# Expert weights split in five pieces a block over 13 blocks instead of eight pieces a block over 8

## The chip, the cores and the metric

One NeuronCore of a Trainium2 chip runs the kernel. The metric is the device time of one execution in microseconds (us), as the median over several executions. A profile is one further execution with the hardware profiler on.

## What is computed

An input x of 16 batches, 256 time steps and 256 features passes four residual layers, x = x + layer(x):

- L0, a tanh recurrence over the time steps: h = tanh(h Wh + x Wx + b)
- L1, an LSTM over the time steps, with four gates of 256
- L2, a mixture of experts: a shared two-matrix feed-forward (256 to 1024 to 256, gelu between) for all, and for each batch the two best of E = 4 experts of the same shape, weighted and masked by segment of time
- L3, an adapter whose low-rank factors w = gelu(c W1 + bias1) W2 + bias2 are generated for each batch from a condition (the "generator"; W2 is 256 by 8192), and that then transforms x

Every fp32 matrix is split into a high and a low fp16 part, and each product is three fp16 products (high by high, low by high, high by low).

## The kernel before

The engines have separate programs, unrolled, which synchronise by semaphores. The sequence of 256 time steps is cut in NB = 16 blocks of U = 16 windows. Window u of block `it` holds one LSTM step, the L0 step of the next block, the input products of later gates (`fig_x`, `o_x`), and a share of the shared feed-forward of block it-1 by the list `FILL`: `shared_hidden` ("h") of tiles 0 to 7 in windows 1, 1, 3, 5, 7, 9, 11, 13, `shared_down` ("d") in the even windows from 2 on. From window to window the LSTM is a loop through three engines: TensorE (PE) makes the gates (L1268, L1274), ScalarE (ACT) takes tanh (L530, L534), VectorE (DVE) updates the cell (L837, L838, L840), ACT takes tanh of the cell (L541), DVE makes the new state (L842), and PE waits for it.

Weights are prepared in the spare time of these windows. SyncE (SP) loads a 1 MB fp32 matrix into a staging buffer. For each piece of 256 columns ACT writes the high part (`weight_hi`, L490) and DVE the low part (`weight_lo`, L722, which then raises the semaphore `v_wlo`). `stage[0]` takes, one after another, the LSTM's first matrix, the shared `sw1` and the eight expert matrices E0 to E7 (`ew1` and `ew2` of four experts, eight pieces each, 64 in all). So expert matrix j can be loaded only when the last piece of matrix j-1 is split. `stage[1]` takes `sw2` and then the eight parts of W2, part j for block j+1: PE multiplies it in windows 12 and 13 (`low_rank`, L1314), DVE adds the bias in window 14 (`add_bias`, which raises `v_low`).

In blocks 1 to 8 one expert matrix a block is split, in windows 2, 4, 5, 6, 7, 9, 11 and 12. ACT waits for the matrix before the first piece of each. All programs are in order: what stands behind a waiting instruction on an engine waits too. In a window ACT has, in order, gate tanh, L0 tanh, cell tanh, refills of gate banks by the bias (`seeds`, in windows 3, 7, 11, 15), gelu (`shared_gelu`, odd windows), a rounding of x (windows 4, 6), and then the piece.

SP's program after the shared matrices is: E0, four bias loads and W2 part 0; then for j = 1 to 7 a wait for the end of W2 part j-1 (`pe_w2`, `v_low`: window 14 of block j), four bias loads (L337), W2 part j (L340), and right behind it E j (L326), whose pieces are by then free. Then, after all splits (`ALL_SPLIT`), the adapter's base matrices and 96 small stores of the generated factors to a scratch in HBM. PE waits for all pieces of the shared matrices (`SHARED_SPLIT`) between block 0 and block 1.

After the 16 blocks come the last shared tiles, the routed experts (which need all expert pieces), and the adapter.

Of the kernel before, what the change touches and what calls it, by code (L numbers as in the profile page):

```python
# [28 lines left out]
C = D // P  # L29
U = 16  # L30
NB = T // U
G = 8
H = 4
E = 4
SHARED = E
F = 1024
M = F // P
# [20 lines left out]
def build_program(nc, a, out, scratch):  # L58
    ctx = ExitStack()
    with ctx:  # L60
# [173 lines left out]
            return stage[0][:, at], S_W1, part_(HI), part_(LO)  # L234


        EXPERT_WINDOWS = (2, 4, 5, 6, 7, 9, 11, 12)

        def x_tiles(half, i):

# [42 lines left out]
        @block.sync  # L283
        def _(sp):
            with nc.allow_non_contiguous_dma(reason="small tables, once"):
                sp.dma_start(cond[:, :], a["cond_1024"]).then_inc(s["ld_cond"], 16)
                wide = lambda w: w.rearrange("(c p) n -> p c n", p=P)

                def load_x(half, quarter):

                    some = slice(4 * quarter, 4 * quarter + 4)
                    sp.dma_start(xin[:, half, some, :], a["x"][some, half * P:(half + 1) * P, :].rearrange("b t d -> t b d")
                                 ).then_inc(s[f"ld_x{half * 4 + quarter}"], 16)

                for quarter in range(4):
                    load_x(0, quarter)
                for w, name in enumerate(("L0_cond_Wx", "L0_cond_Wh")):
                    sp.dma_start(rnn_raw[:, w], wide(a[name])).then_inc(s["ld_rnn"], 16)
                sp.wait_ge(s["g_const"], 3)
                for row in (0, 32):  # L300
                    sp.dma_start(bias_rows[row:row + 1, 0:4 * D],
                                 a["L1_cond_b"].rearrange("(a n) -> a n", a=1)).then_inc(s["ld_bias"], 16)
                    sp.dma_start(bias_rows[row:row + 1, 4 * D:5 * D],
                                 a["L0_cond_b"].rearrange("(a n) -> a n", a=1)).then_inc(s["ld_bias"], 16)
                for w, name in enumerate(("L1_cond_Wx", "L1_cond_Wh")):
                    sp.dma_start(stage[w][:, :].rearrange("p (c n) -> p c n", c=C), wide(a[name])
                                 ).then_inc(s[f"ld_stage{w}"], 16)
                for quarter in range(4):
                    load_x(1, quarter)
                for i, tile in enumerate(FIG_TILES + O_TILES):  # L310
                    sp.dma_start(gate_bias[:, i:i + 1], a["L1_cond_b"][tile * P:(tile + 1) * P].rearrange("(p o) -> p o", o=1)
                                 ).then_inc(s["ld_gate_bias"], 16)
                small_tables(sp)
                sp.wait_ge(s["v_wlo"], N_RNN + N_LSTM // 2)
                sp.dma_start(stage[0][:, :].rearrange("p (c n) -> p c n", c=C), wide(a["L2_cond_sw1"])
                             ).then_inc(s["ld_stage0"], 16)
                sp.wait_ge(s["v_wlo"], LSTM_SPLIT)
                sp.dma_start(stage[1][:, :].rearrange("p (m n) -> p m n", m=M), wide(a["L2_cond_sw2"])
                             ).then_inc(s["ld_stage1"], 16)

                for j in range(2 * E):
                    def load_expert():

                        sp.wait_ge(s["v_wlo"], SHARED_SPLIT + j * N_MATRIX if j else LSTM_SPLIT + N_MATRIX)
                        src = a[("L2_cond_ew1", "L2_cond_ew2")[j % 2]][j // 2]
                        sp.dma_start(stage[0][:, :].rearrange("p (c n) -> p c n", c=(C, M)[j % 2]), wide(src)  # L326
                                     ).then_inc(s["ld_stage0"], 16)

                    if j == 0:
                        load_expert()  # L330
                        sp.wait_ge(s["v_wlo"], SHARED_SPLIT)
                    else:
                        sp.wait_ge(s["pe_w2"], j)
                        sp.wait_ge(s["v_low"], j)
                    for t in range(4):
                        at = j * 1024 + t * LOW_N
                        sp.dma_start(low_bias[32 * t:32 * t + 32, :],  # L337
                                     a["L3_cond_bias2"][at:at + LOW_N].partition_broadcast(2 * B)
                                     ).then_inc(s["ld_bias2"], 16)
                    sp.dma_start(w2_in, wide(a["L3_cond_W2"])[:, :, j * 1024:(j + 1) * 1024]  # L340
                                 ).then_inc(s["ld_stage1"], 16)
                    if j > 0:
                        load_expert()
                sp.wait_ge(s["v_wlo"], ALL_SPLIT)
                for dst, name in ((down, "L3_cond_base_down"), (up, "L3_cond_base_up")):
                    sp.dma_start(dst, wide(a[name])).then_inc(s["ld_updown"], 16)

                sp.wait_ge(s["a_low"], Q * C)
                sp.wait_ge(s["v_lowlo"], Q * C)
                for g in range(Q * C):  # L350
                    for place, h in enumerate((HI, LO, HI) if g // C in LEFT else (HI, HI, LO)):
                        for t in range(4):
                            at = g % C * P + t * LOW_D
                            dst = scratch[place, :, g // C, at:at + LOW_D].rearrange("(b r) d -> b r d", r=R)
                            sp.dma_start(dst, rows[32 * t:32 * t + B, h, g]).then_inc(s["st_scratch"], 16)
                sp.wait_ge(s["st_scratch"], N_SCRATCH)

            def load_low(b, r):
                sp.dma_start(low[r], scratch[:, bass.ds(b * R, R), :, :].rearrange("h r q d -> h r (q d)")
                             ).then_inc(s[f"ld_low{r}"], 16)  # L360

            def store_out(b, slot):
                sp.wait_ge(s["a_out"], b * 2 + 2)
                sp.dma_start(out[bass.ds(b, 1), :, :].rearrange("o (k p) d -> p (o k) d", p=P),
                             y4[:, slot]).then_inc(s[f"st_out{slot}"], 16)

            def step(b, r, prev, this, next1, next2):
                if not isinstance(b, int) or b + 4 < B:
                    sp.wait_ge(s["pe_e1"], b + 1)
                    load_low(b + 4, r)  # L370
                if prev:
                    store_out(b - 1, (r + 1) % 2)

            for b in range(4):
                load_low(b, b)
            adapter_steps(sp, step)
            for slot in range(2):
                sp.wait_ge(s[f"st_out{slot}"], 16 * (B // 2))
# [98 lines left out]
        def _(act):  # L477
# [9 lines left out]
            def weight_hi(piece):  # L487

                view, scale, hi, _lo = piece
                nc.scalar.activation(hi, view, ACT.Copy, scale=scale).then_inc(s["a_whi"], 1)  # L490
# [101 lines left out]
            def block_steps(it, first, last, matrix=False):  # L592
                for u in range(U):
# [16 lines left out]
                        weight_hi(shared_piece(i))  # L610
                    if matrix and u == HI_WINDOW:
                        low_hi(it - 1)
                    if matrix and u in EXPERT_WINDOWS:
                        i = EXPERT_WINDOWS.index(u)
                        if i == 0:
                            act.wait_ge(s["ld_stage0"], it * 16 + 32)
                        weight_hi(expert_piece(it - 1, i))

            def low_hi(g):

# [77 lines left out]
        def _(dve):  # L698
# [247 lines left out]
            def block_steps(it, first, last, xr, matrix=False):  # L946
                for u in range(U):
# [13 lines left out]
                        add_bias(it - 1)  # L961
                    if matrix and u == LO_WINDOW:
                        low_lo(it - 1)
                    if matrix and u in EXPERT_WINDOWS:
                        i = EXPERT_WINDOWS.index(u)
                        weight_lo((it - 1) * N_MATRIX + (SHARED_SPLIT + i), expert_piece(it - 1, i))
                    if xr and u in X_LO:
                        x_lo(it + 2, X_LO.index(u))
                    if last and u == U - 4:
# [196 lines left out]
        def _(pe):  # L1166
# [126 lines left out]
            def shared_hidden(blk, m):  # L1293
                tile = blk * M + (M + m)
                def free():
                    if m == 0:
                        pe.wait_ge(s["v_x2p"], blk * 2 + (4 if blk == NB - 1 else 2))
                    pe.wait_ge(s["a_g"], tile - 1)
                hidden(tile, lambda h, c: SW1[:, h, c, m * P:(m + 1) * P],
                       lambda h, c: XHL[:, h, c, :, bass.ds(blk * U, U)], HB[m % 2], free)  # L1300

            def shared_down(blk, m):
                if m == 0:
                    pe.wait_ge(s["v_y"], blk + 1)
                down_(blk * M + (M + m), m, lambda h, c: SW2[:, h, m, c * P:(c + 1) * P],
                      m == 0, m == M - 1, YB)

# [129 lines left out]
                    rnn_x(it + 2)  # L1437

            block_steps(0, True, False, True)
            pe.wait_ge(s["v_wlo"], SHARED_SPLIT)  # L1440
            for it in range(1, 2 * E + 1):
                block_steps(it, False, False, True, matrix=True)
            for it in range(2 * E + 1, NB - 2):
# [161 lines left out]
```

## Time and profile before

| what | value |
|---|---|
| median of 3 runs | 1182.06 us (1181.74 to 1182.39) |
| profiled execution, its own time | 1186.63 us |
| profiled execution, span from first to last instruction | 1184.8 us |
| PE busy | 1136.6 us, 96% |
| DVE busy | 766.9 us, 65% |
| ACT busy | 608.0 us, 51% |
| mean granted TensorE clock | 0.960 |
| expert loads: 8 of 1024 KB, median time from issue to landing | 8.6 us |
| W2 loads: 8 of 1024 KB, the same | 5.4 us |

The 1.8 us between span and time of the profiled execution lie outside its instructions. Its time is 4.6 us over the median of the runs.

### The profile page before, as it was taken

How to read it: one execution, taken by the hardware profiler on the slowest of the kernel's cores; microseconds unless marked ns; L12 is line 12 of the kernel's file. 1: busy time of each engine (PE TensorE's matmuls, PEld its weight loads, DVE VectorE, ACT ScalarE, POOL GpSimd, SP SyncE). 2: the span in 40 equal slices, each digit the busy share in tenths (PEclk: the TensorE clock that was granted, in tenths of full speed). 3: DMA queues.
4: the chain of work that ended last, by engine and by line, in shares of the span. 5: the costliest groups of instructions: out<-in, count | busy, mean ns of one | idle time of the engine just before them, and what ended most of it. 6: DMA issues, size and time to landing. Idle time of an engine off the chain costs nothing. (4 is left out here: it accounts for less than half of the span.)

```text
span 1184.8 us, 58156 instructions
## 1 busy us (share of the span) xinstructions
PE 1136.6 (96%) x23706; PEld 1014.0 (86%) x23706; DVE 766.9 (65%) x2954; ACT 608.0 (51%) x2147; POOL 364.4 (31%) x1372
## 2 busy tenths in 40 slices
PE   5899999999999999999999999899999999999898
PEld 4788888888889888999999998678888888888687
DVE  6566666666666666565565657687666666666697
ACT  4456566566566565555565554533333333333476
POOL 3654344344434344444444440063000000000121
PEclk7759999989989999999999999899999999999899
DMA  8211202202102011110000000000000000000022
GB/s 243 74 44 39 79 4 80 79 4 79 53 31 79 29 54 26 14 15 12 5 4 4 5 4 4 3 1 2 2 2 2 2 1 2 2 2 2 5 75 86
DMA packets 44432, 37.14 MB, mean 31 GB/s; under 512 B 24280, under 2 KB 39946, under 8 KB 44172
## 3 DMA queue, kind: packets, MB, share of 16 engines
q1 hardware_dynamic: 43564, 33.12, 9.2%
q8 instruction: 194, 3.18, 1.1%
q14 instruction: 66, 0.54, 0.2%
q10 hardware_dynamic: 608, 0.30, 0.1%
HBM read 28.42 MB, written 4.98 MB: 28 GB/s over the span
## 5 line engine op out<-in xcount | busy, mean ns | idle before, releaser
L1268 PEld LDWEIGHTS bank<-LH,seq 128*128 128x128 f16 x8192 | 248.8, 96 | 54.0 <-DVE LH L842 46.5
L1268 PE MATMUL bank<-LH,seq 128*128 128x16 f16 x8192 | 283.1, 170 | 12.3 <-DVE LH L842 10.3
L568 ACT ACTIVATE gel<-bank,seq 128x256 f32<-128x256 f32 x256 | 121.5, 475 | 215.0 <-PE bank L1173 211.3
L1171 PE MATMUL bank<-XHL,WE 128*128 128x256 f16 x768 | 210.6, 274 | 5.7 <-issue 2.9
L1171 PE MATMUL bank<-GH,WE 128*128 128x256 f16 x768 | 210.6, 274 | 2.2 <-DVE GH L815 1.8
L1172 PE MATMUL bank<-XHL,WE 128*128 128x256 f16 x768 | 210.7, 274 | 0.0
L1173 PE MATMUL bank<-XHL,WE 128*128 128x256 f16 x768 | 210.7, 274 | 0.0
L1172 PE MATMUL bank<-GH,WE 128*128 128x256 f16 x768 | 210.7, 274 | 0.0
L1173 PE MATMUL bank<-GH,WE 128*128 128x256 f16 x768 | 210.6, 274 | 0.0
L1274 PE MATMUL bank<-LH,seq 128*128 128x16 f16 x4096 | 177.2, 169 | 2.3 <-issue 2.3
L399 POOL TENSOR_TENSOR RH<-rf,RH 128x32 f16<-128x32 f32 x256 | 64.6, 252 | 355.9 <-ACT RH L525 355.9
L530 ACT ACTIVATE tfig<-bank 128x96 f32<-128x96 f32 x256 | 65.8, 257 | 210.4 <-PE bank L1274 208.2
L822 DVE CAST GH<-gel 128x256 f16<-128x256 f32 x256 | 78.3, 306 | 103.7 <-ACT gel L568 102.9
L1274 PEld LDWEIGHTS bank<-LH,seq 128*128 128x128 f16 x4096 | 139.5, 96 | 1.6 <-issue 1.6
L1172 PE MATMUL bank<-seq 128*128 128x64 f16 (+2 forms) x960 | 138.6, 207 | 1.4 <-issue 1.4
L1173 PE MATMUL bank<-seq 128*128 128x64 f16 (+2 forms) x960 | 139.7, 207 | 0.0
L1171 PE MATMUL bank<-seq 128*128 128x64 f16 (+2 forms) x960 | 137.1, 206 | 0.0
L469 POOL TENSOR_TENSOR seq<-X,seq 128x512 f16<-128x512 f32 x16 | 19.3, 1205 | 342.2 <-ACT seq L643 342.2
L837 DVE SCALAR_TENSOR_TENSOR fc<-tfig,c 128x32 f32<-128x32 f32 x256 | 48.9, 191 | 114.8 <-ACT tfig L530 109.5
L824 DVE TENSOR_TENSOR GH<-gel,GH 128x256 f16<-128x256 f32 x256 | 113.0, 441 | 8.7
L842 DVE SCALAR_TENSOR_TENSOR LH<-to,tc 128x32 f16<-128x32 f32 x256 | 51.7, 202 | 78.3 <-ACT tc L541 78.3
L1173 PEld LDWEIGHTS bank<-seq 128*128 128x128 f16 x960 | 91.4, 100 | 2.8 <-issue 1.5
(193 smaller groups left out, 2539.6 us busy)
## 6 DMA issues: line engine op xcount, KB each, us to landing
stage<-in_L_cond_ew SPq DMA_DIRECT2D x8, 1024.0 KB, 8.6
stage<-in_L_cond_W SPq DMA_DIRECT2D x8, 1024.0 KB, 5.4
XHL<-in_x SPq DMA_DIRECT2D x8, 512.0 KB, 9.0
out<-WE SPq DMA_DIRECT2D x16, 256.0 KB, 2.1
stage<-in_L_cond_sw SPq DMA_DIRECT2D x2, 1024.0 KB, 5.5
scratch<-rows SPq DMA_DIRECT2D x96, 8.0 KB, 2.3
stage<-in_L_cond_Wx SPq DMA_DIRECT2D x1, 1024.0 KB, 9.1
stage<-in_L_cond_Wh SPq DMA_DIRECT2D x1, 1024.0 KB, 11.3
```

Of the source, the lines that this page charges most:

```text
L399: nc.gpsimd.tensor_tensor(RH[:, slot, LO], rf[:, slot], RH[:, slot, HI], ALU.subtract).then_inc(s["p_rlo"], 1)
L530: nc.scalar.activation(tfig[:], FIG[u // H % 2][:, 0:6 * H * B].rearrange("p (m t b) -> p m t b", m=6, t=H)[:, :, u % H, :], ACT.Tanh, sca ...
L568: nc.scalar.activation(gel[:, m % 2, :], banks[m % len(banks)][:, 0:256], ACT.Gelu_apprx_tanh, scale=scale, bias=bias).then_inc(s["a_g"], 1)
L822: V.tensor_copy(GH[:, m % 4, HI], gel[:, m % 2]).then_inc(s["v_gh"], 1)
L824: V.tensor_tensor(GH[:, m % 4, LO], gel[:, m % 2], GH[:, m % 4, HI], ALU.subtract).then_inc(s["v_gl"], 1)
L837: V.scalar_tensor_tensor(fc[:], tf, 1.0, c2[:], ALU.add, ALU.mult)
L842: V.scalar_tensor_tensor(hh, to[:], 1.0, tc[:], ALU.add, ALU.mult).then_inc(s["v_hh"], 1)
L1171: MM(out_, w(HI), x(HI), start=start, stop=False, skip_group_check=True)
L1172: MM(out_, w(LO), x(HI), start=False, stop=False, skip_group_check=True)
L1173: return MM(out_, w(HI), x(LO), start=False, stop=stop, skip_group_check=True)
L1268: MM(z, LW[:, h, 1, c, tile * P:(tile + 1) * P], LH[:, old, HI, c], start=False, stop=False, skip_group_check=True)
L1274: last = MM(z, LW[:, HI, 1, c, tile * P:(tile + 1) * P], LH[:, old, LO, c], start=False, stop=(c == C - 1), skip_group_check=True)
```

## The change

`EXPERT_WINDOWS` becomes (2, 4, 7, 9, 11): the pieces of windows 5, 6 and 12 are gone, and the 64 pieces are numbered through. Piece i is split in block i // 5 + 1, window `EXPERT_WINDOWS[i % 5]`, so blocks 1 to 12 have five pieces each and block 13 has four. A matrix ends in the middle of a block. ACT waits for a new one before each piece i with i % 8 == 0.

SP's order is built by a loop over blocks: expert matrix j stands ahead of the W2 part of the block in which its first piece can be split. The order is E0, W0, W1, E1, W2, W3, E2, W4, E3, W5, W6, E4, W7, E5, E6, E7 (Wj: part j of W2 with its bias loads). The waits of each load are unchanged: E j for the last piece of E j-1, W j for the use of W j-1.

PE's wait for both shared matrices between blocks 0 and 1 is taken out. `shared_hidden` of block 0 waits for the first (`LSTM_SPLIT + N_MATRIX`), `shared_down` of block 0 for the second.

```diff
-        EXPERT_WINDOWS = (2, 4, 5, 6, 7, 9, 11, 12)
+        EXPERT_WINDOWS = (2, 4, 7, 9, 11)
+        PIECES = 2 * E * N_MATRIX
...
-                for j in range(2 * E):
-                    def load_expert():
+                def load_expert(j):
...
-                    if j == 0:
-                        load_expert()
                         sp.wait_ge(s["v_wlo"], SHARED_SPLIT)
...
-                    if j > 0:
-                        load_expert()
+                loaded = 0
+                for it in range(NB - 1):
+                    while loaded < 2 * E and (loaded * N_MATRIX - 1) // len(EXPERT_WINDOWS) + 1 <= it:
+                        load_expert(loaded)
+                        loaded += 1
+                    if it < 2 * E:
+                        load_low_matrix(it)
...
-                    if matrix and u in EXPERT_WINDOWS:
-                        i = EXPERT_WINDOWS.index(u)
-                        if i == 0:
-                            act.wait_ge(s["ld_stage0"], it * 16 + 32)
-                        weight_hi(expert_piece(it - 1, i))
+                    if it > 0 and u in EXPERT_WINDOWS:
+                        i = (it - 1) * len(EXPERT_WINDOWS) + EXPERT_WINDOWS.index(u)
+                        if i < PIECES:
+                            if i % N_MATRIX == 0:
+                                act.wait_ge(s["ld_stage0"], i // N_MATRIX * 16 + 48)
+                            weight_hi(expert_piece(i // N_MATRIX, i % N_MATRIX))
...
+                            weight_lo(SHARED_SPLIT + i, expert_piece(i // N_MATRIX, i % N_MATRIX))
...
+                    if blk == 0 and m == 0:
+                        pe.wait_ge(s["v_wlo"], LSTM_SPLIT + N_MATRIX)
...
+                    if blk == 0:
+                        pe.wait_ge(s["v_wlo"], SHARED_SPLIT)
...
             block_steps(0, True, False, True)
-            pe.wait_ge(s["v_wlo"], SHARED_SPLIT)
```

## Rows read from the trace of the kernel before

**Rows 1.** Windows by block 2, 7, 8, 10: length, busy, clock, DMA share, GB/s.

```profile
core 0: us, PE busy (x) PEld busy (x) DVE busy (x) ACT busy (x) POOL busy (x), PEclk, DMA share, GB/s
136.30:183.60 47.30, 45.18 (x1262) 40.58 (x1259) 29.82 (x138) 27.67 (x114) 19.26 (x80) 0.96 0.16 51
...
370.10:414.70 44.60, 44.16 (x1262) 39.76 (x1259) 29.83 (x137) 27.66 (x114) 19.01 (x80) 1.00 0.15 54
414.70:461.90 47.20, 44.30 (x1261) 39.81 (x1258) 29.82 (x137) 27.64 (x114) 18.99 (x80) 1.00 0.14 46
...
504.70:547.40 42.70, 42.53 (x1244) 39.60 (x1241) 25.49 (x127) 24.56 (x104) 18.95 (x80) 1.00 0.12 18
```

**Rows 2.** Timeline of SP: start, duration, load.

```profile
85.36 1.72 SPq L337 DMA_DIRECT2D low_bias<-in_L_cond_bias  x4
...
131.23 1.71 SPq L337 DMA_DIRECT2D low_bias<-in_L_cond_bias  x4
132.98 0.43 SPq L340 DMA_DIRECT2D stage<-in_L_cond_W  x1
133.46 0.47 SPq L326 DMA_DIRECT2D stage<-in_L_cond_ew  x1
178.48 1.80 SPq L337 DMA_DIRECT2D low_bias<-in_L_cond_bias  x4
...
223.96 2.84 SPq L337 DMA_DIRECT2D low_bias<-in_L_cond_bias  x4
...
271.91 3.08 SPq L337 DMA_DIRECT2D low_bias<-in_L_cond_bias  x4
...
317.33 2.03 SPq L337 DMA_DIRECT2D low_bias<-in_L_cond_bias  x4
...
365.07 1.72 SPq L337 DMA_DIRECT2D low_bias<-in_L_cond_bias  x4
...
409.65 1.73 SPq L337 DMA_DIRECT2D low_bias<-in_L_cond_bias  x4
```

**Rows 3.** Waits of PE from 93 to 460 us: total, times, longest.

```profile
PE bank L1171 <- issue: 2.5, 1, 2.5
...
PE bank L1248 <- issue: 1.7, 1, 1.7
```

**Rows 4.** DMA queues from 131 to 138.4 us, then from 138.4 to 140.5 us.

```profile
DMA packets 739, 1.46 MB, mean 198 GB/s; under 512 B 80, under 2 KB 483, under 8 KB 739
...
q1 hardware_dynamic: 739, 1.46, 69.7%
...
q8 instruction: 1, 0.02, 2.8%
```

**Rows 5.** Waits of PE's weight loads for the LSTM state, from 93 to 460 us.

```profile
PEld bank L1268 <- DVE LH L842: 22.3, 73, 0.7
```

**Rows 6.** Timeline of PE at the first LSTM step of block 1.

```profile
90.26 0.82 PE L1268 MATMUL bank<-LH,seq 128*128 128x16 f16 x24
```

**Rows 7.** Timeline of DVE, starts of windows 5 and 11, block 7 and block 10.

```profile
383.24 0.19 DVE L837 SCALAR_TENSOR_TENSOR fc<-tfig,c 128x32 f32<-128x32 f32 x1 [0.42 <-ACT tfig L530]
...
399.06 0.19 DVE L837 SCALAR_TENSOR_TENSOR fc<-tfig,c 128x32 f32<-128x32 f32 x1 [0.34 <-ACT tfig L530]
...
517.77 0.19 DVE L837 SCALAR_TENSOR_TENSOR fc<-tfig,c 128x32 f32<-128x32 f32 x1 [0.96 <-ACT tfig L530]
...
532.97 0.19 DVE L837 SCALAR_TENSOR_TENSOR fc<-tfig,c 128x32 f32<-128x32 f32 x1 [0.44 <-ACT tfig L530]
```

**Rows 8.** Issues of the expert loads from 66 to 70 us: E0 alone.

```profile
DMA to landing us min/median/max: 5.6/5.6/5.6
```

**Rows 9.** Timelines of DVE and ACT, block 2: end of window 7, window 9.

```profile
159.97 0.42 DVE L722 SCALAR_TENSOR_TENSOR WE<-stage,WE 128x256 f16<-128x256 f32 x1
...
164.64 0.41 ACT L490 ACTIVATE WE<-stage 128x256 f16<-128x256 f32 x1
164.95 0.25 ACT L530 ACTIVATE tfig<-bank 128x96 f32<-128x96 f32 x1
```

**Rows 10.** The same in block 7: end of window 2, window 4.

```profile
377.40 0.44 DVE L722 SCALAR_TENSOR_TENSOR WE<-stage,WE 128x256 f16<-128x256 f32 x1
...
381.96 0.40 ACT L490 ACTIVATE WE<-stage 128x256 f16<-128x256 f32 x1
382.96 0.25 ACT L530 ACTIVATE tfig<-bank 128x96 f32<-128x96 f32 x1 [0.59 <-PE bank L1274]
```

More of the change, by code:

```diff
@@ L319, in _, with load_low_matrix @@
                              ).then_inc(s["ld_stage1"], 16)
-                for j in range(2 * E):
-                    def load_expert():
[L324 to L327, printed above, removed]
+                def load_expert(j):
+                    sp.wait_ge(s["v_wlo"], SHARED_SPLIT + j * N_MATRIX if j else LSTM_SPLIT + N_MATRIX)
+                    src = a[("L2_cond_ew1", "L2_cond_ew2")[j % 2]][j // 2]
+                    sp.dma_start(stage[0][:, :].rearrange("p (c n) -> p c n", c=(C, M)[j % 2]), wide(src)
+                                 ).then_inc(s["ld_stage0"], 16)
+                def load_low_matrix(j):
                     if j == 0:
-                        load_expert()
                         sp.wait_ge(s["v_wlo"], SHARED_SPLIT)
@@ L963, in block_steps @@
                         low_lo(it - 1)
-                    if matrix and u in EXPERT_WINDOWS:
-                        i = EXPERT_WINDOWS.index(u)
-                        weight_lo((it - 1) * N_MATRIX + (SHARED_SPLIT + i), expert_piece(it - 1, i))
+                    if it > 0 and u in EXPERT_WINDOWS:
+                        i = (it - 1) * len(EXPERT_WINDOWS) + EXPERT_WINDOWS.index(u)
+                        if i < PIECES:
+                            weight_lo(SHARED_SPLIT + i, expert_piece(i // N_MATRIX, i % N_MATRIX))
                     if xr and u in X_LO:
```

## Prediction

> **What bounds the kernel now.** I read the busy time by block first. In blocks 7 and 10 PE is busy for all but 0.4 and 0.2 us of the block, while ACT and DVE stand at about 60% [rows 1]. That makes PE look like the only bound. The waits correct it: in blocks 1 to 8 PE's weight loads waited 73 times for the LSTM state, 22.3 us together [rows 5]. So the loop from PE over ACT and DVE back to PE has almost no slack in most windows, and a delay of ACT or DVE inside the loop comes out as time unless the window has idle ACT time in front of the gate tanh. Where it has, is read from the timeline, window by window.
>
> Next come the blocks' lengths, from SP's timeline: the bias loads start at window 14 of each block, so their distances are block periods. They are 47.25, 45.48, 47.95, 45.42, 47.74 and 44.58 us [rows 2]. The work of these blocks is the same (1259 to 1262 matmuls, about 29.8 us of DVE and 27.7 us of ACT in blocks 2, 7 and 8 [rows 1]), yet they differ by up to 3.4 us. Against the best, 44.58, the five others lose 2.67 + 0.90 + 3.37 + 0.84 + 3.16 = 10.9 us. Block 8 lies behind the last of these rows; its length is 47.20 against 44.60 of block 7, 2.6 more [rows 1]. Together 13.5 us.
>
> Where do they go? The waits of PE name "issue": 2.5 us in one piece, 1.7 us in another [rows 3]. PE has no instruction to run, and no engine keeps it. The DMA view shows why. From 131 to 138.4 us, while W2 part 1 and E1 are in flight one right behind the other (issued at 132.98 and 133.46 [rows 2]), all 739 packets are those of the kernel's own loads, and not one is an instruction packet; one comes in the 2.1 us after that [rows 4]. I read it so: PE's instructions come in by DMA too, their packet stands in line behind 2 MB of weights, and PE runs dry for 1.7 us [rows 3]. After the stall the granted clock of block 2 is 0.96 instead of 1.00, and PE's busy time 45.18 instead of 44.16 [rows 1]: a stretch at 1.2 GHz instead of 2.4, which costs 1.0 us more.
>
> One rule of the Trainium skill speaks against this reading. "Runtime: NRT & Kernel Launch", section Instruction fetch mechanics, says that instructions are fetched ahead in 16 KiB blocks on a queue of their own, and that the fetch is hidden. By that rule nothing would be won from the order of the loads, and the sum below would be 12.0 us higher. The trace shows the issue waits, so here I do not follow it, and keep it as a rival.
>
> **The change part by part.**
>
> *PE's wait at the end of block 0: 0.* Both shared matrices are split when SP issues its first bias load, 85.36 us [rows 2], because that load waits for the same count. PE starts block 1 at 90.26 us [rows 6], 4.9 us later. The wait ended nothing, and the two that take its place are met as early.
>
> *Loads one at a time: -13.5, of which 1.5 stay.* In the new order the expert loads hang on the end of a matrix in the middle of a block and W2 at window 14. Place of each: piece 7 is block 2 window 7, piece 15 block 4 window 2, piece 23 block 5 window 9, piece 31 block 7 window 4, piece 39 block 8 window 11, piece 47 block 10 window 7, piece 55 block 12 window 2. None is within two windows (5 us) ahead of, or behind, window 14. SP's queue doesn't hold one back behind the other either: at each place the load before it in the queue is due earlier. So each load is 1 MB alone. The trace doesn't show what a lone load does to PE in blocks 1 to 8. Lower bound nothing: E0, alone, had landed after 5.6 us [rows 8] against a median of 8.6. Upper bound: each of the seven W2 loads costs the 0.84 us of the mildest pair, 5.9. I take two such hits, about 1.5, nearer to nothing, since the pairs of the period of 44.58 cost nothing although they too were 2 MB. Net -12.0.
>
> *Pieces of windows 5, 6, 12 gone from eight blocks: -1.7.* From window 5 to window 11 block 7 takes 399.06 - 383.24 = 15.82 us, block 10 without pieces 532.97 - 517.77 = 15.20 [rows 7]. The 0.62 us belong to pieces in windows 5, 6, 7 and 9. In odd windows ACT has the two gelus ahead of the piece and the gate tanh right behind it without idle time [rows 9]; in even ones there is idle time (0.59 us in window 4 [rows 10]). So I give it to the three odd ones, 0.21 each. Windows 6 and 12 give nothing. 8 x 0.21 = 1.7. Bounds: nothing, and 8 x 3 x 0.21 = 5.0.
>
> *Pieces into blocks 9 to 13: +2.9.* 24 of the 64 pieces. Windows 2 and 4 are free by the same reading. Windows 7, 9 and 11 in blocks 9 to 12, and 7 and 9 in block 13: 14 x 0.21 = 2.9. PE is no cover for them: block 10's period has 0.2 us without PE. Bounds: nothing, and 24 x 0.21 = 5.0.
>
> *ACT waits for matrices in mid-block: +5.8.* This is the part that the old order didn't have: there a matrix was ordered at window 14 and wanted at window 2. Now five matrices are wanted two windows after the last piece of the one before. E1, E3 and E6: last piece in an odd window, first new one two windows on. The low part ends at 159.97 + 0.42 = 160.39, and ACT stands at the next but one piece at 164.64 [rows 9], 4.25 us later; a lone load needs 5.6 [rows 8]. ACT stands still for 1.35 us, with the gate tanh of the next window right behind (the DVE's cell, its low part and PE's next step wait for that). Nothing covers it: 3 x 1.35 = 4.05. E2 and E7, window 2 to window 4: from 377.84 to 381.96 is 4.12 us, ACT waits 1.48, of which the idle 0.59 takes up a part [rows 10]: 2 x 0.89 = 1.8. E4 (window 4 to 7) has some 8 us and E5 (window 11 to the next block) more: nothing. Bounds: nothing if a load lands in 4.2 us, and 5 x 1.48 = 7.4 if no idle time helps.
>
> *Clock after these five waits: +1.5.* PE has nothing to do for 0.9 to 1.3 us each time. The stall of 1.7 us was followed by a stretch at the lower clock, price 1.0 us; that of 2.5 us in block 8 was not (clock 1.00 [rows 1]). I take one or two in five. Bounds 0 and 5.
>
> *SP's later work.* The base matrices and 96 small stores now come after block 13, window 9, and not after block 8. They then lie beside blocks 13 to 15. Their old neighbours are blocks 9 to 11, and block 10 ran with them at clock 1.00 and PE busy for 42.53 of 42.70 us [rows 1]. They cost nothing there, and nothing here; their readers come only after the 16 blocks.
>
> **Sum:** 0 - 12.0 - 1.7 + 2.9 + 5.8 + 1.5 = -3.5 us. In the profiled execution, 1186.6 to 1183.1 (span 1184.8 to 1181.3). The runs without profiler take 1182.06, so 1178.6.
>
> **Rivals.**
>
> - *The waits cost more than I say* (chance 0.20): each of the five brings a slow-clock stretch, or lasts to the upper bounds: 5 - 1.5 = 3.5 more, 1182.1. For it speaks the lack of slack [rows 5], against it that block 8's longer stall had no such stretch.
> - *The pairs cost less without profiler, or lone loads still starve PE* (0.15). [...] The place is the fetch of PE's instructions at window 14 to 3. If only 5 of the 13.5 us come back, the sum is -5 - 1.7 + 2.9 + 5.8 + 1.5 = +3.5: 1185.6, slower. It decides from a recovery under 8.5 us (no gain) and under 6.1 us (slower than the measurement's limit).
> - *The fetch is hidden anyway and the issue waits have another cause that stays* (0.05): -1.7 + 2.9 + 5.8 + 1.5 = +8.5, 1190.6. The packet-free 7.4 us [rows 4] speak against it.
> - *The load waits are hidden* (0.10): a lone load lands in time, or the loop catches up: -3.5 - 5.8 - 1.5 = -10.8, 1171.3. The 5.6 us of E0 [rows 8] speak against it.
> - My forecast, 0.50, alone 1176 to 1181.
>
> **How the numbers follow.** About 0.2% (2.4 us) is what a measurement can tell from no change. Faster is below 1179.7: four fifths of the forecast's 0.50, the 0.10 of hidden waits, a little of the first rival: 0.53. Slower is above 1184.4: the 0.05, most of the 0.15: 0.18. The rest, 0.29, is within. The range has to reach over both signs: 1174 leaves out most of the hidden waits, 1186 the hidden fetch and part of the smaller recovery.
>
> **What the profile will show.** Block periods in blocks 2 to 8 even, at about 44.4 us plus 1.3 us in those with a wait; "issue" rows of PE gone or under 1 us; landing of all expert loads near 5.6 us. A wait of ACT's L490 for the expert load, five times, 1.3 to 1.5 us. Blocks 9 to 12 at 43.3 us and not 42.7. Wrong it is if issue waits persist beside lone loads, if ACT's waits don't lengthen the window, or if the clock falls after each.

## The result and the profile after

The changed kernel takes 1188.41 us (median of 5 runs, 1186.85 to 1189.04) against 1182.39: a ratio of 1.0043, 95% interval 1.0022 to 1.0064. By the ratio it is slower by 5 us (by these medians 6), and the forecast was 3.5 us faster. On a second occasion it was 1187.67 against 1182.96, 1.0042 (1.0023 to 1.0061), over 12 and 23 runs.

The blocks of the profiled execution (its own time 1188.41, span 1186.6 us), in the view by windows: block 2, block 5, block 6, block 10, block 11. Columns as in [rows 1].

```profile
core 0: us, PE busy (x) PEld busy (x) DVE busy (x) ACT busy (x) POOL busy (x), PEclk, DMA share, GB/s
135.30:181.90 46.60, 44.12 (x1261) 39.88 (x1258) 28.75 (x134) 26.59 (x111) 19.06 (x80) 1.00 0.17 52
273.40:323.50 50.10, 47.58 (x1261) 41.48 (x1258) 28.57 (x135) 26.89 (x110) 19.68 (x80) 0.90 0.19 60
323.50:367.90 44.40, 43.99 (x1261) 39.80 (x1258) 28.81 (x135) 26.73 (x110) 18.98 (x80) 1.00 0.08 21
501.00:545.10 44.10, 42.88 (x1244) 39.46 (x1241) 27.14 (x132) 25.59 (x109) 19.03 (x80) 1.00 0.09 28
545.10:588.60 43.50, 42.90 (x1244) 39.48 (x1241) 27.20 (x132) 25.66 (x109) 18.93 (x80) 1.00 0.02 4
```

Blocks 6 and 11 are as forecast: 44.40 us where block 7 took 44.60 [rows 1], 43.5 where block 10 took 42.7. Blocks with a load wait stand out, and block 5 most: 5.7 us over block 6, at a mean clock of 0.90.

Waits of the same execution: PE from 93 to 460 us, then ACT from 93 to 720 us.

```profile
PE bank L1277 <- DVE LH L850: 5.0, 10, 1.2
PE bank L1182 <- issue: 2.1, 1, 2.1
PE bank L1257 <- issue: 0.9, 1, 0.9
PE bank L1251 <- issue: 0.8, 1, 0.8
PE bank L1181 <- issue: 0.6, 1, 0.6
```

```profile
ACT WE L497 <- DMA stage<-in_L_cond_ew: 6.4, 5, 2.1
```

The single issue waits of 2.5 and 1.7 us [rows 3] are gone, but one of 2.1 has come, and with those of 0.9, 0.8 and 0.6 us (each during a lone load or just behind one) PE still waits 4.4 us for instructions, where it was 8.6 in the same view of before. By the forecast's own signs ("issue" rows under 1 us) this is a miss. ACT stands still five times, 6.4 us in all; the forecast had 3 x 1.35 + 2 x 1.48 = 7.0 before counting the idle time of ACT in window 4.

The wait in block 5 and what follows. ACT first (last piece of E2 in window 9, first of E3 in window 11; gaps in a listing are marked by dots), then SP's load of E3, then the starts of windows 10 to 15 and of the next block on DVE.

```profile
298.87 0.41 ACT L497 ACTIVATE WE<-stage 128x256 f16<-128x256 f32 x1
...
305.28 0.42 ACT L497 ACTIVATE WE<-stage 128x256 f16<-128x256 f32 x1 [1.09 <-DMA stage<-in_L_cond_ew]
305.60 0.23 ACT L537 ACTIVATE tfig<-bank 128x96 f32<-128x96 f32 x1
```

```profile
299.80 0.39 SPq L326 DMA_DIRECT2D stage<-in_L_cond_ew  x1
```

```profile
299.68 0.18 DVE L845 SCALAR_TENSOR_TENSOR fc<-tfig,c 128x32 f32<-128x32 f32 x1
302.12 0.19 DVE L845 SCALAR_TENSOR_TENSOR fc<-tfig,c 128x32 f32<-128x32 f32 x1 [0.34 <-ACT tfig L537]
306.07 0.18 DVE L845 SCALAR_TENSOR_TENSOR fc<-tfig,c 128x32 f32<-128x32 f32 x1
310.55 0.19 DVE L845 SCALAR_TENSOR_TENSOR fc<-tfig,c 128x32 f32<-128x32 f32 x1 [3.01 <-ACT tfig L537]
314.87 0.19 DVE L845 SCALAR_TENSOR_TENSOR fc<-tfig,c 128x32 f32<-128x32 f32 x1 [1.06 <-ACT tfig L537]
319.61 0.19 DVE L845 SCALAR_TENSOR_TENSOR fc<-tfig,c 128x32 f32<-128x32 f32 x1 [2.82 <-ACT tfig L537]
323.49 0.19 DVE L845 SCALAR_TENSOR_TENSOR fc<-tfig,c 128x32 f32<-128x32 f32 x1 [0.61 <-ACT tfig L537]
```

Read it as differences. Window 11 takes 306.07 - 302.12 = 3.95 us, where block 6 has 2.78: the wait, 1.2 us, as priced. But windows 12 to 15 take 4.48, 4.32, 4.74 and 3.88 us, where block 6 has 2.85, 3.01, 3.36 and 3.68: 4.5 us more, though ACT waits for no load in them. Two things make them longer, and PE's timeline shows the first:

```profile
304.81 0.19 PE L1181 MATMUL bank<-seq 128*128 128x64 f16 x1
307.12 0.20 PE L1182 MATMUL bank<-seq 128*128 128x64 f16 x1 [2.12 <-issue]
...
308.09 1.08 PE L1327 MATMUL bank<-stage,hidT 128*32 128x256 f32 x8
```

The issue wait of 2.1 us stands here, in the middle of the products that PE has behind its LSTM step, and at its end PE still has 1.0 us of them to do. `low_rank` (L1327) starts 2.02 us after the start of window 12, in block 6 0.90 us after it: 1.1 of the 4.5 us. The DMA queues say what PE waited for, from 298 to 304.6 us and from there to 307.2:

```profile
q1 hardware_dynamic: 1022, 1.04, 50.8%
...
q8 instruction: 1, 0.02, 2.6%
```

In the first stretch all 1022 packets are those of loads, in the second comes the instruction packet. I read it as in [rows 4]: the load that ACT waits for, alone as it is, also held back PE's instructions. In the second profile of the changed kernel the same wait stands at the same instruction, 1.96 us. The clock is the second thing, in the view by windows:

```profile
303.00:308.00 5.00, 2.88 (x81) 2.41 (x78) 2.51 (x13) 2.23 (x9) 2.10 (x10) 1.00 0.32 113
308.00:318.00 10.00, 10.00 (x174) 6.95 (x173) 3.47 (x17) 3.76 (x13) 2.28 (x10) 0.50 0.02 5
```

Half of 2.4 GHz for these 10 us, and PE busy for every one of them. The clock fell 0.9 us after the 2.1 us in which PE had nothing to do.

### The profile page after: what moved, and what is told of

The parts are those of the page before. It is cut to its first block and busy times, and to the rows that moved or that the text cites. A ratio compares the mean times of both kernels' runs of the same rounds, so it can differ in the third digit from the quotient of the medians.

```text
span 1186.6 us, 58155 instructions
## 1 busy us (share of the span) xinstructions
PE 1139.5 (96%) x23706; PEld 1014.9 (86%) x23706; DVE 766.0 (65%) x2954; ACT 605.0 (51%) x2147; POOL 363.6 (31%) x1372
## 5 line engine op out<-in xcount | busy, mean ns | idle before, releaser
L1181 PE MATMUL bank<-seq 128*128 128x64 f16 (+2 forms) x960 | 138.4, 206 | 0.0
```

Of the source, the lines that this page charges most:

```text
L1181: MM(out_, w(LO), x(HI), start=False, stop=False, skip_group_check=True)
```

## The experiments

**The kernel before again, with a new profile.** Edit: none.

> The kernel before, unchanged, with a new profile. Theory A (the profiled execution of before was not a typical one: its stalls of PE beside the paired loads and the slow-clock stretches after them cost more than in the timed runs): the time is again near 1182.3 us, and a profile of an execution of that time has block periods from 131 us on that lose clearly less than the 13.5 us that I read, 8 to 10 us, with fewer stretches at the lower clock. Theory B (the profiler itself costs the 4.6 us, evenly): the profiled execution is again some 4 us over the timed ones, with the same block periods.

Time 1180.57 us against 1181.99 (ratio 0.9988, 0.9968 to 1.0007); the profiled execution is the quickest, 1177.19 us. Its blocks 2, 4, 7 and 8 by windows:

```profile
135.70:183.00 47.30, 45.13 (x1260) 40.57 (x1257) 29.68 (x137) 27.64 (x113) 19.26 (x80) 0.96 0.16 51
228.30:273.60 45.30, 44.13 (x1259) 39.84 (x1256) 29.75 (x137) 27.66 (x113) 19.23 (x80) 1.00 0.17 53
366.00:410.60 44.60, 44.16 (x1261) 39.76 (x1258) 29.85 (x138) 27.66 (x114) 19.00 (x80) 1.00 0.16 55
410.60:457.60 47.00, 44.28 (x1260) 39.78 (x1257) 29.81 (x138) 27.62 (x113) 19.00 (x80) 1.00 0.14 47
```

Blocks 2 and 8 lose what they lost before. The period around block 4 took 47.95 in the execution that I read [rows 2], and block 4 takes 45.3 here. From the starts of the windows, blocks 2 to 8 lose 9.8 us here, not 13.5. The profiled execution is not slow (3.4 us under the median of its 12 runs), so theory B falls. Of theory A the first half holds: the stalls come back, the stretches at the lower clock after them only in part (6.8 us of them in blocks 1 to 8 here, 17.1 in the first profile). That the first profile was not typical is not shown. A third profile with the same order of loads, that of PE's waits alone below, is of an execution of 1183.77 us, near the median of before on its occasion (1182.96), and its blocks 2 to 8 lose 14.5 us. Nor do the 9.4 us between the times of the first two executions lie mostly in the counted stalls: 3.8 are in blocks 1 to 8, and 5.1 from the start of block 15 to the end, which takes 467.9 us in one and 462.8 in the other.

**Gaps at the matrix boundaries.**

```diff
+        SLOT, at_ = {}, 0
+        for i_ in range(PIECES):
+            if i_ % N_MATRIX == 0 and i_:
+                w_ = EXPERT_WINDOWS
+                if w_[at_ % 5] - w_[(at_ - 1) % 5] == 2:
+                    at_ += 1
+            SLOT[at_] = i_
+            at_ += 1
...
-                        i = (it - 1) * len(EXPERT_WINDOWS) + EXPERT_WINDOWS.index(u)
-                        if i < PIECES:
+                        i = SLOT.get((it - 1) * len(EXPERT_WINDOWS) + EXPERT_WINDOWS.index(u))
+                        if i is not None:
```

> The changed kernel with one empty piece window at each matrix boundary where the next piece would come two windows later, so that a load has 8 us and more. Theory A (ACT's waits for the matrices in mid-block and the slow clock that follows them cost 5.8 us and 3 to 5 us): 8 to 10 us under the changed kernel, 1178 to 1181 us, with no wait of ACT for an expert load left. Rival (the waits lie in slack, and the pieces in 13 blocks or the lone loads cost it): within 2 us of the changed kernel, 1187 to 1190 us.

1173.23 us, ratio to before 0.9923 (0.9897 to 0.9950): 14 us under the changed kernel, more than I expected. Three empty windows move the other boundaries off too. No wait of ACT for an expert load is left, and blocks 3 to 7 take 44.2 to 44.4 us each. The windows that hold the five waits were 5.8 us too long in the first profile of the changed kernel, so most of the other 8 us lay behind them. Both kinds of idle time of PE went together, though: in this profile its issue waits from 93 to 460 us are 1.0 us in all, not 4.4, and none stands in block 5. The gaps moved the loads against PE's program.

**The loads apart, nothing else.**

```diff
+                    load_expert()
                     if j == 0:
-                        load_expert()
                         sp.wait_ge(s["v_wlo"], SHARED_SPLIT)
...
-                    if j > 0:
-                        load_expert()
```

> The kernel before with one part of the change alone: the loads apart. In each block SP issues the expert matrix ahead of the W2 part, when its last piece is split (window 12), and the W2 part at window 14 as before. Eight pieces a block, eight blocks, PE's wait as before. Forecast's theory (pairs of loads starve PE, lone loads hardly): 12 us under before, 1170 us. Theory A (the same, but a typical execution loses less): 5 to 9 us under before, 1173 to 1177. Rival (lone loads starve PE as much, or the issue waits have another cause): 0, 1182 us.

1172.28 us, ratio 0.9923 (0.9894 to 0.9952): 9 us under before by the ratio, with an interval of 5.7 to 12.5. SP's timeline shows the load of E at window 12 and the W2 part at window 14; the waits of PE from 93 to 460 us show what lone loads do:

```profile
125.48 0.38 SPq L326 DMA_DIRECT2D stage<-in_L_cond_ew  x1
131.28 1.72 SPq L337 DMA_DIRECT2D low_bias<-in_L_cond_bias  x4
133.05 0.43 SPq L340 DMA_DIRECT2D stage<-in_L_cond_W  x1
```

```profile
PE bank L1266 <- DVE LH L840: 3.1, 8, 0.4
PE bank L1246 <- issue: 0.6, 1, 0.6
PE bank L1169 <- issue: 0.5, 1, 0.5
```

The same bytes, and PE starves for 1.1 us; in before the issue waits of this view are 8.6 us in all, of which [rows 3] shows the two longest single ones. The expert loads land after 5.5 us (median) where they took 8.6.

**Other traffic in the pair's place.** A copy that nobody needs behind each W2 part of the kernel above.

```diff
+    extra = nc.dram_tensor("extra", (8, 256, 1024), F32, kind="Internal").ap()
...
+                    if j > 0:
+                        sp.dma_start(extra[j], a["L2_cond_ew1"][0]).then_inc(s["ld_extra"], 16)
```

> The kernel of e3_expert_first (loads apart, 1172.3 us) with a copy of 1 MB from HBM to HBM, which no one waits for until the end, issued right behind each of the seven later W2 parts, so in the place that the expert load had in the kernel before. Theory of the fetch (2 MB ahead of PE's instruction packets make it run dry, whatever the bytes are for): issue waits of 1.5 to 2.5 us return in blocks 2, 4, 6 and 8, and the kernel goes back most of the way to before, 8 to 12 us over e3. Rival (it was the write into SBUF, or a conflict with the engines' own accesses): no change, 1172 us.

1185.15 us, ratio to before 1.0019 (1.0002 to 1.0036): 11 us over the kernel with the loads apart by the ratios (13 by the medians, of two occasions). Waits of PE from 93 to 460 us:

```profile
PE bank L1270 <- DVE LH L844: 3.1, 8, 0.4
PE bank L1276 <- issue: 3.1, 2, 2.2
PE bank L1173 <- issue: 2.8, 1, 2.8
PE bank L1270 <- issue: 1.4, 1, 1.4
```

The copy touches no SBUF and no engine waits for it, and the issue waits are back. What counts is the traffic and not what it is for. Whether the instruction packet stands behind it in the DMA engines or at HBM, which the copy uses too, these runs can't tell.

**The pieces in even windows.**

```diff
-        EXPERT_WINDOWS = (2, 4, 7, 9, 11)
+        EXPERT_WINDOWS = (2, 4, 8, 10, 12)
```

> The changed kernel with its five pieces in windows 2, 4, 8, 10 and 12 and not 2, 4, 7, 9 and 11. The third to fifth piece leave the odd windows, where the gelus stand ahead of them. The matrix boundaries still have two windows between them in most places, one more of them than before (31 to 32 has four). Forecast's price of a piece in an odd window (0.21 us, 38 pieces): 8 us less, and about 1.5 us less for waits that meet 0.6 us of idle time: 1179 us. Rival (odd and even windows cost the same): 1187 to 1189 us.

1178.85 us, ratio to before 0.9968 (0.9948 to 0.9988), 9 us under the changed kernel. Block 9 by windows, with its five pieces:

```profile
451.40:494.20 42.80, 42.63 (x1247) 39.70 (x1244) 27.32 (x133) 26.11 (x110) 19.56 (x80) 1.00 0.02 4
```

As long as a block without any piece (42.70 [rows 1]): in even windows they cost nothing. ACT's five waits were still there, 7.2 us in all. One of them cost nothing, in window 12 of block 5, where PE has the products of `low_rank`:

```profile
307.62 0.42 ACT L497 ACTIVATE WE<-stage 128x256 f16<-128x256 f32 x1 [1.66 <-DMA stage<-in_L_cond_ew]
```

That block takes 43.97 us from window 0 to window 0; block 6, without a wait, takes 43.99. What a wait costs depends on the window it falls in.

**Gaps and even windows.** Both edits together.

> Both cures together: pieces in windows 2, 4, 8, 10 and 12, and an empty piece window at a matrix boundary that would be two windows wide. No wait of ACT for a load, no piece behind the gelus. From the windows measured so far: under the kernel with the gaps alone (1173.2 us) by 38 pieces at 0.21 to 0.26 us, 8 to 9 us, so 1164 to 1166 us. If odd pieces only were dear because of the waits next to them: 1172 to 1174.

1168.87 us, ratio 0.9891 (0.9865 to 0.9916): the fastest version, 13 us under before and 18 under the changed kernel by the ratios, though 3 us over the range that I expected. Its profile has one stretch at the lower clock, in block 7, behind an issue wait of PE of 1.1 us (waits of PE from 93 to 720 us, block 7 by windows):

```profile
PE bank L1260 <- issue: 1.1, 1, 1.1
```

```profile
356.00:402.10 46.10, 44.78 (x1260) 40.64 (x1257) 28.61 (x134) 26.84 (x109) 19.44 (x80) 0.96 0.16 52
```

**The changed kernel again.** Edit: none.

> The changed kernel again, with a new profile, beside the kernel before on the same chip. If the slow-clock stretches behind ACT's five waits belong to the change (6.5 us of windows longer than clean ones in its first profile, 4.5 of them in windows 12 to 15 of block 5), they return here at the same places and the kernel is 4 to 7 us over before. If they were a chance of that execution, windows 12 to 15 of block 5 have their clean lengths, the block periods sum up to 4 to 5 us less, and the kernel stands at the level of before, within 2 us.

1187.67 against 1182.96 us. Block 5 in its profile, the start of windows 11 to 14 on DVE:

```profile
304.22 0.19 DVE L845 SCALAR_TENSOR_TENSOR fc<-tfig,c 128x32 f32<-128x32 f32 x1 [0.35 <-ACT tfig L537]
308.19 0.18 DVE L845 SCALAR_TENSOR_TENSOR fc<-tfig,c 128x32 f32<-128x32 f32 x1
313.23 0.19 DVE L845 SCALAR_TENSOR_TENSOR fc<-tfig,c 128x32 f32<-128x32 f32 x1 [3.57 <-ACT tfig L537]
316.23 0.19 DVE L845 SCALAR_TENSOR_TENSOR fc<-tfig,c 128x32 f32<-128x32 f32 x1 [0.55 <-ACT tfig L537]
```

The wait is again 1.2 us (window 11: 3.97). The stretch is shorter: window 12 takes 5.04 instead of 2.85, window 13 its clean 3.0. In exchange block 2 has a stretch, which it had not before: it takes 48.3 us, not 46.6. Over all windows the time above clean ones behind the waits is 6.5 us in the first profile and 6.1 in the second; part of it, in blocks 4 and 5, is the work that the missing instructions put off. Stretches behind these waits are in both profiles; their length and place vary.

**One wait alone.** The gap kernel with other empty windows, so that one boundary is two windows wide.

```diff
-                w_ = EXPERT_WINDOWS
-                if w_[at_ % 5] - w_[(at_ - 1) % 5] == 2:
-                    at_ += 1
+                at_ += {1: 1, 2: 4, 6: 1}.get(i_ // N_MATRIX, 0)
```

> The kernel with gaps, but with exactly one mid-block wait put back: matrix E3 ends in window 9 of block 6 and is followed by E4's first... that is, the fourth expert matrix (E3) is wanted two windows after the end of E2, in window 11 of block 6; all other boundaries are three windows or wider. Clock theory (a wait of this size, here, brings a stretch at 1.2 GHz): window 11 of block 6 is 1.2 us longer and windows 12 to 15 together 3 to 5 us longer than in the other blocks; 4 to 6 us over the kernel with gaps. Rival (the wait costs its 1.2 us and nothing follows): 1.2 us over it.

1177.29 us, ratio to before 0.9940 (0.9919 to 0.9962). Start of windows 10 to 13 of block 6:

```profile
340.75 0.18 DVE L852 SCALAR_TENSOR_TENSOR fc<-tfig,c 128x32 f32<-128x32 f32 x1
...
343.19 0.19 DVE L852 SCALAR_TENSOR_TENSOR fc<-tfig,c 128x32 f32<-128x32 f32 x1 [0.34 <-ACT tfig L544]
...
347.17 0.18 DVE L852 SCALAR_TENSOR_TENSOR fc<-tfig,c 128x32 f32<-128x32 f32 x1
...
349.60 0.19 DVE L852 SCALAR_TENSOR_TENSOR fc<-tfig,c 128x32 f32<-128x32 f32 x1 [0.97 <-ACT tfig L544]
```

The wait is there (window 11 from 343.19 to 347.17: 3.98 us), and the clock does not fall; the next window even gives 0.4 back. But no issue wait stands beside this one, and PE itself is idle for less than in block 2 or 5 of the changed kernel, as its waits from 93 to 720 us show:

```profile
PE bank L1284 <- DVE LH L857: 7.6, 23, 0.7
```

So this profile shows that a wait of ACT of 1.1 us need not bring a stretch; it does not test a gap of 1 us or more in PE's own work. The timed kernel lies 2 us over the gap kernel by the ratios (0.9940 against 0.9923), with intervals that overlap.

**The same waits, but PE busy in them.**

```diff
+        BUSY = ((2, 11), (4, 6), (5, 13), (10, 11), (12, 6))
...
+                    if (it, u) in BUSY:
+                        for _ in range(10):
+                            MM(YB[:, 0:256], bias_pad[64:128, 0:P], ones_pad[64:128, 0:256], start=False, stop=False,
+                               skip_group_check=True)
```

> The changed kernel with ten added matmuls of 256 columns (zeros added to a sum, 1.07 us at 2.4 GHz) ahead of PE's LSTM step in the five places where PE stands idle because ACT waits for an expert matrix: block 2 window 11, block 4 window 6, block 5 window 13, block 10 window 11, block 12 window 6. The waits themselves stay. Clock theory (PE's idle time in the waits brings the stretches at 1.2 GHz, which cost 6 us of the changed kernel's time): the waits are as long as before, the stretches between block 1 and block 12 go, and the kernel is 4 to 6 us under the changed one, 1182 to 1184 us. Rival (the stretches have another cause, or the added work only lengthens the windows): at or over the changed kernel, 1187 to 1192 us.

1184.49 us, ratio to before 1.0018 (1.0001 to 1.0036), against 1.0042 of the changed kernel: 3 us less, for 5 us more work of PE, though the intervals overlap (the other is 1.0023 to 1.0061). The waits of ACT are even longer in its profile, and block 5 (by windows) keeps the full clock:

```profile
ACT WE L498 <- DMA stage<-in_L_cond_ew: 7.5, 5, 2.5
```

```profile
275.00:320.60 45.60, 45.18 (x1272) 40.67 (x1269) 28.64 (x134) 26.71 (x110) 19.03 (x80) 1.00 0.19 55
```

45.6 us instead of 50.1 and 47.8. A stretch is left behind the wait in block 12, where PE had to wait for longest. Over the 12 timed runs the mean granted clock is 0.969 (median), for the changed kernel 0.9605, for before 0.965 and 0.967 on the two occasions. Those clocks are means over the whole kernel: of the 31 us at the lower clock that this profile has less than the first one of the changed kernel, 10 lie in blocks 1 to 14. And block 5 is not a clean case, because the added matmuls moved PE's program against the loads: its issue wait of 2.1 us is gone too. So the result fits PE's idle time as the cause, and does not tell ACT's wait from the missing instructions. The gain was under the 4 to 6 us that I expected.

**All twelve profiles together.** In blocks 1 to 14 they have 26 stretches at the lower clock. Each begins during an idle gap of PE or within 3 us of its end; 21 times PE lacked instructions in it, 5 times the LSTM state. Ten other gaps of PE, from 0.8 up to 2.45 us, were followed by none. In the two profiles of the changed kernel:

| wait of ACT | PE idle, us (i: all or part of it issue) | stretch after it, us |
|---|---|---|
| block 2 | 1.2; 1.3 | none; 6.8 |
| block 4 | 1.5 (i); 1.3 (i) | 3.4; 3.4 |
| block 5 | 2.1 (i); 2.0 (i) | 10.2; 3.4 |
| block 10 | 0.6; 0.6 | none; none |
| block 12 | 1.0; 1.3 | 3.4; none |

Where a stretch stands alone its price is even: 1.0 us in blocks 4 and 12 of the first profile (3.4 us long), 1.9 in block 2 of the second (6.8 us long).

**PE's waits alone.** Only the three edits of `shared_hidden`, `shared_down` and the line between blocks 0 and 1.

> The kernel before with one part of the change alone: PE's wait for both shared matrices between block 0 and block 1 replaced by the two waits in the first shared products. All theories: 0; in the profile the last window of block 0 and the first three of block 1 have the lengths of the kernel before (6.2, 2.5, 3.1, 2.5 us), since the awaited count is reached 4 to 5 us before PE gets there.

1182.79 us, ratio 0.9990 (0.9973 to 1.0008). SP's bias load, which waits for the same count, goes out at 86.74 us, and PE starts block 1 at 90.71; windows 0 to 2 of block 1 take 2.5, 3.1 and 2.5 us, as expected. The last window of block 0 took 5.2 us in this profile and not 6.2; of the profiles with the moved waits four show 4.9 to 5.2 us there and four 6.1 to 6.2, as all four without them do. In the short ones the stretch at the lower clock over block 0 ends a microsecond earlier, ahead of the last input products; that the wait has to do with it can't be told from so few, and the times show nothing of it.

## Why the prediction was wrong

Step by step, forecast against what the runs showed:

| step | forecast | measured | from |
|---|---|---|---|
| PE's wait moved | 0 | 0 | PE's waits alone |
| loads apart, net | -12.0 | -9 (-5.7 to -12.5) timed; -8.3 and -12.0 by profile | loads apart; before again and before: 9.8 and 13.5, less 1.5 |
| windows 5, 6, 12 | -1.7 | -1.5 | block 6: 44.40 against 44.60, eight blocks |
| pieces in blocks 9 to 13 | +2.9 | +3.7 | 43.5 against 42.7, five blocks, the last with fewer |
| ACT's five waits | +5.8 | +5.8 | the windows that hold them, first profile |
| clock after them | +1.5 | +6.5 and +6.1, missing instructions included | windows behind them, two profiles |
| sum | -3.5 | about +5 | ratio 1.0043 |

The differences of the terms are 3 + 0.2 + 0.8 + 0 + 4.8 = 8.8 us; the forecast was off by 5.0 + 3.5 = 8.5.

**The step that failed is the clock after the five waits**, in its size: 1.5 us forecast, 6.5 and 6.1 measured. I had its mechanism and the price of a stretch, but took "one or two in five". Six of ten waits were followed by one, and they are 3.4 to 10.2 us long, where the one that I had priced at 1.0 us was 3.4 us long. Block 5 alone cost 4.5 us behind its wait, and 2.2 the second time. There the forecast missed a link between two of its own terms: ACT waits for an expert load, so that load is in flight, and while it is, PE's instructions may not come. PE stood still there for 2.1 and 2.0 us, and not for 0.9 to 1.3. That "each load is 1 MB alone" was right and did not prevent it. The kernel with gaps, 14 us faster where the windows of the waits hold 5.8, shows from the outside that more lay behind them, but it removed both kinds of idle time at once.

What stays open is why a gap in PE's work of about the same length is followed by a stretch one time and not the next (block 2: 1.2 and 1.3 us; block 12: 1.0 and 1.3), and how the 4.5 us of block 5 would divide without the issue wait: no run has the one without the other there.

**The gain of the loads apart** was right in kind; its size can't be faulted with certainty. Forecast were 12.0 us, timed 9, with an interval that reaches 12.5. I took the 13.5 us from one execution whose own time was 4.6 us over the median, and carried the whole sum over to the median; two more profiles of this order of loads give 9.8 and 14.5. The 1.5 us for lone loads stood in the kernel with the loads apart (1.1 us of issue waits). In the changed kernel, where loads start in mid-block, the issue waits are 4.4 and 4.2 us. So a part of the rival that lone loads still starve PE came true, and so did one of the forecast's own signs of being wrong.

That rival, with the smaller recovery, gave 1185.6 us and got 0.15; the rival of dearer waits named the clock with 1182.1. They held together, and neither alone reaches 1188: I treated as alternatives what could add up, and the range ended at 1186.

What stands: the reading of the issue waits. By the rule of the Trainium skill ("Runtime: NRT & Kernel Launch", Instruction fetch mechanics) nothing was to be won from the order of the loads; moving one load two windows ahead won 9 us, and a useless copy in its place lost them again. The prices of the pieces and of the waits stood to within a microsecond, though single waits scattered (0.6 us in block 10, 1.7 in block 4).

So the change traded one kind of stall for another: PE waiting for instructions behind paired loads, 9 us, against ACT waiting for a matrix ordered two windows before, 5.8 us, with a rest of the first kind beside it, and stretches at the lower clock follow both. With the second kind taken out by three empty windows, and the pieces moved away from the gelus, its idea is worth 13 us (0.9891).

## What to carry to other kernels

In a loop through several engines without slack, a load wait of 1.2 us can cost more than its length: in six of ten cases here PE ran at half its clock for 3 to 10 us behind it, at about 1 us for each 3.4. See that no such wait is there, by ordering a transfer earlier than it takes to land (5.5 us for 1 MB here). Look at PE's own idle time, and not only at the wait of the engine in front of it. Keep large transfers apart when an engine executes a long unrolled program, because its instructions come by DMA too. A load on its own can still hold them back: for 2.1 us here, where ACT was waiting for just that load. And before a sum is made from one profile, take a second one and compare them stage by stage: two executions of the kernel before differ by 9.4 us, 3.8 of them in the stalls that I had counted as gain and 5.1 in a stage that the change does not touch.

## What the runs showed of the hardware that was not expected

- The time of one execution follows the mean granted clock: over 23 runs of the kernel before on one chip, 1177.9 us at 0.971 to 1187.5 at 0.960. A spread of 10 us needs no change in the program.
- A copy of 1 MB from HBM to HBM, touching no SBUF, starves PE of instructions as much as a weight load (issue waits of 2.8 and 2.2 us).
- A lone load of 1 MB did it as well, at one place: 2.1 and 2.0 us in block 5 of the changed kernel.
- In blocks 1 to 14 of twelve profiles PE never left the full clock without an idle gap of PE just before (26 stretches); ten gaps of 0.8 to 2.45 us were followed by none.
- Ten matmuls that add zeros, put in each of five places where PE would stand idle, did not make the kernel slower; it was rather faster (1.0018 against 1.0042, intervals that overlap).
